# Cross-attention of the last layer: where VectorE joins, normalises and carries the first batch of a pair

## The reference

```python
def _mha(x, y, ...):                      # second call: y = ee, causal=False
    xn = _ln(x, lnx_g, lnx_b)
    yn = _ln(y, lny_g, lny_b)
    q = jnp.einsum('bsc,hcd->bhsd', xn, wq)
    ...
    a = jax.nn.softmax(jnp.einsum('bhsd,bhtd->bhst', q, k) * D ** (-0.5), axis=-1)
    o = jnp.einsum('bhst,bhtd->bhsd', a, v)
    ...
    x_out = x + o @ li1_w + li1_b
    h = jax.nn.gelu(_ln(x_out, ln3_g, ln3_b) @ li2_w + li2_b, approximate=False)
    return x_out + h @ li3_w + li3_b
...
x = _ln(x, ln2_g, ln2_b)
return x + _mha(x, ee, a2_wq, ...)
```

## Time and profile before

| what | value |
|---|---|
| median of 3 runs | 3002.09 us (2995.72 to 3003.3) |
| the profiled execution's own time | 3003.06 us |
| its span in the trace | 3001.4 us |
| PE busy | 2444.2 us (81%) |
| DVE busy | 1303.4 us (43%) |
| ACT busy | 889.5 us (30%) |
| POOL busy | 683.4 us (23%) |

### The profile page before, as it was taken

The page is one execution under the profiler, slowest core; times in us unless marked ns, Lnnn a source line. Parts: engine busy times, 40 slices in busy tenths (PEclk is TensorE's granted clock), DMA queues, the critical chain, the costliest instruction groups (busy, mean ns, idle before and its releaser), DMA issues.

```text
span 3001.4 us, 32215 instructions
## 1 busy us (share of the span) xinstructions
PE 2444.2 (81%) x11498; PEld 1621.5 (54%) x11498; DVE 1303.4 (43%) x2740; ACT 889.5 (30%) x1980; POOL 683.4 (23%) x767
## 2 busy tenths in 40 slices
PE   6898888987688299977899799999783299999925
PEld 3555554555366177753446554446462168888703
DVE  6664465634555311115673536573526023333205
ACT  3453254533341022213553225562310011111100
POOL 3052220122012400013111320002311702222270
PEclk9899999998798599988999899999795699999967
DMA  9000000000002322200000000000001315555430
GB/s 361 16 1 1 1 1 1 1 1 0 7 1 106 143 88 94 95 32 14 15 15 1 0 1 1 1 1 1 1 0 74 117 57 197 197 199 197 142 101 28
DMA packets 64402, 173.28 MB, mean 58 GB/s; under 512 B 6608, under 2 KB 45136, under 8 KB 56208
## 3 DMA queue, kind: packets, MB, share of 16 engines
q0 software_dynamic: 21280, 95.11, 9.2%
q1 hardware_dynamic: 43008, 76.66, 7.1%
HBM read 121.81 MB, written 49.94 MB: 57 GB/s over the span
## 4 chain that ended last, share of the span: by engine, by line
PE 70%; DVE 13%; another core or an unknown queue 5%; issue 5%; ACT 4%; POOL 2%; DMA 0%; DVEq 0%; ACTq 0%; SPq 0%; POOLq 0%
PE PS L2175 8%; PE PS L982 6%; PE PS L973 6%; PE PS L576 5%; PE PS L1950 5%; PE PS L1964 5%; PE PS L2189 4%; PE PS L606 4%; PE PS L932 3%; PE PS L517 3%; PE PS L556 2%; PE PS L2090 2%; DVE arena L680 2%; PE PS L1162 2%
## 5 line engine op out<-in xcount | busy, mean ns | idle before, releaser
L637 ACT ACTIVATE arena<-PS,arena 128x512 f32<-128x512 f32 (+3 forms) x512 | 306.4, 606 | 207.5 <-DVE arena L680 173.1
L680 DVE TENSOR_REDUCE arena<-PS 128x1 f32<-128x512 f32 (+3 forms) x512 | 273.4, 584 | 137.3 <-PE PS L582 82.9
L576 PE MATMUL PS<-arena 64*128 64x512 f32 (+3 forms) x1024 | 294.6, 567 | 32.4 <-ACT arena L637 21.8
L2175 PE MATMUL PS<-arena 128*128 128x256 f32 (+1 forms) x1128 | 252.1, 379 | 0.9 <-DVE arena L2213 0.9
L2175 PEld LDWEIGHTS PS<-arena 128*128 128x128 f32 (+1 forms) x1128 | 203.4, 180 | 40.7 <-issue 1.1
L288 POOL TENSOR_TENSOR arena<-arena 128x4 f32<-128x4 f32 x45 | 47.6, 1057 | 761.1 <-DVE arena L299 370.9
L2090 PE MATMUL PS<-arena 128*128 (+1 forms) x192 | 96.8, 661 | 142.4 <-issue 93.6
L606 PE MATMUL PS<-arena 128*128 128x128 f32 x1280 | 174.1, 281 | 17.0 <-ACT arena L637 12.8
L576 PEld LDWEIGHTS PS<-arena 64*128 64x128 f32 x1024 | 104.0, 187 | 143.9 <-ACT arena L637 93.9
L606 PEld LDWEIGHTS PS<-arena 128*128 128x128 f32 x1280 | 140.9, 144 | 71.7 <-ACT arena L637 47.3
L861 POOL TENSOR_TENSOR arena<-arena 128x512 f32<-128x512 f32 (+2 forms) x108 | 88.9, 827 | 381.2 <-ACT arena L832 375.6
(11 more groups left out here) (344 smaller groups left out, 3967.9 us busy)
## 6 DMA issues: line engine op xcount, KB each, us to landing
arena<-e SPq DMA_DIRECT2D x8, 2048.0 KB
arena<-slots SPq DMA_DIRECT2D x55, 256.0 KB, 2.7
yslots<-arena POOLq DMA_DIRECT2D x55, 256.0 KB, 7.8
slots<-zeros SPq DMA_DIRECT2D x1, 12032.0 KB, 39.6
slots<-zeros SPq DMA_DIRECT2D x1, 5120.0 KB, 34.9
arena<-w3a SPq DMA_DIRECT2D x1, 4106.0 KB, 13.5
arena<-w3b SPq DMA_DIRECT2D x1, 3593.0 KB, 21.6
arena<-slots SPq DMA_DIRECT2D x8, 384.0 KB
```

Of the source, the lines that this page charges most:

```text
L576: ins = nc.tensor.matmul(PS[:, hh, 0:w], q[:, t * P:(t + 1) * P], k[:, 0:w], start=True, stop=not cfg["causal"])
L637: nc.scalar.activation(PRB[m % 6][:, 0:w], PS[:, hh, 0:w], ACT.Exp, bias=nmax[:, m:m + 1], accum_out=rsum[:, col:col + 1]).then_inc(s["pro ...
L680: nc.vector.tensor_reduce(nmax[:, m:m + 1], PS[:, hh, 0:w], AX, ALU.max, negate=True).then_inc(s["nmax"], 1)
L2175: ins = nc.tensor.matmul(PS[0:n, 2 * c + up, 0:BN], wbuf3[i][:, off:off + n], xsT3[i][:, k, :], start=k == 0, stop=k == KC - 1)
```

## The change

In batch z's cross-attention (and in what follows it) VectorE's list is changed in four ways. The join of batch a stands ahead of the first shift, not behind it. The second shift is ahead of the moments. The normalisation of batch a is VectorE's own, behind the fourth shift (`third_scaled`), and that of batch z is too. `carried(a)` stands behind the sum of batch z. GpSimd keeps only the power of -0.5 for the two, without a wait for the sums.

```diff
--- before.py
+++ after.py
@@ -2522,9 +2522,9 @@
                 pool_norm(pool, N3("f2", z))
                 biased(1, z, "a2li1b", "a2li3b")
                 folded(z, range(1))
-                third(1, a)
+                pool_norm(pool, N3("f3", a))
                 folded(z, range(1, QT))
-                third(1, z)
+                pool_norm(pool, N3("f3", z))
                 if a + 2 < B:
                     pool_norm(pool, N3("ln1", a + 2))
                     scaled("f0", 0, a + 2, tiles_of(x1s[0]), xns[0])
@@ -2595,6 +2595,14 @@
                 x1 = x1s[b % 2]
                 V.tensor_tensor(x1, x1, xns[b % 2], ALU.add).then_inc(own["summed"], 1)
                 v.wait_ge(own["summed"], X3(stage, b) + 1)
+
+            def third_scaled(b):
+                v.wait_ge(norm["rstd"], N3("f3", b) + 1)
+                to = xns[b % 2]
+                for t in range(QT):
+                    ins = V.tensor_scalar(to[:, t, :], to[:, t, :], mv[:, 2 * t:2 * t + 1], rstd[:, t:t + 1],
+                                          ALU.subtract, ALU.mult)
+                ins.then_inc(xf["xn_ready"], 1)
 
             def carried(b):
                 xr = X[:, b * QT:(b + 1) * QT, :]
@@ -2663,20 +2671,22 @@
                 turned_x(2, z, c3c)
                 dve_cross_y(v, sc_, a + 2 * B, c3c, ch)
                 dve_cross_q(v, sc_, z + 2 * B, c3c)
+                joined(2, a)
                 shift(z, 0)
-                joined(2, a)
+                shift(z, 1)
                 third(1, a)
-                shift(z, 1)
                 summed(1, a)
                 shift(z, 2)
-                carried(a)
                 shift(z, 3)
+                third_scaled(a)
                 dve_cross_shares(v, sc_, z + 2 * B, c3c, ch, folds3)
                 turned_x(3, a, c3g)
                 dve_cross_y(v, sc_, z + 2 * B, c3c, ch)
                 joined(2, z)
                 third(1, z)
                 summed(1, z)
+                carried(a)
+                third_scaled(z)
                 turned_x(3, z, c3g)
                 carried(z)
                 if a + 2 < B:
```

## The result

| | before | changed |
|---|---|---|
| median, 7 runs each | 3001.44 us (2995.72 to 3003.3) | 2990.18 us (2984.78 to 2991.28) |
| ratio | | 0.9959, 95% interval 0.9948 to 0.997 |
| profiled execution, its span | 3003.06, 3001.4 us | 2984.78, 2983.1 us |
| first shift to feed-forward (L885 to L973), first pair | 31.87 us | 25.27 us |
| the same, second pair | 32.13 us | 25.13 us |

The account below looks back on a forecast made before the run. Bound taken: VectorE's last shift waiting for GpSimd's fold behind its scalings, on the ending chain twice. Earlier shifts 13.0 plus clock 2.0 gave 15.0 us off 3003.06; median 2987.0 us, range 2980 to 2995 (0.80).

Parts of the forecast that it names:

- The fold behind the scalings: Batch z's cross-attention: GpSimd's fold of tile 1, queued behind four scalings (5.87 us), holds VectorE's last shift.
- The join: VectorE, moved ahead of the first shift into idle time: gain 0 to 0.1 us, taken as 0.
- The last shift: VectorE, batch z's cross-attention: starts 6.5 to 7.2 us earlier, taken as 6.9; second pair 6.0 to 7.2, taken as 6.1.
- the base of the sum: Gain from the earlier last shifts in both pairs: 6.9 + 6.1 = 13.0 us.
- The scaling on VectorE: Scalings at 408 ns, at most 1.6 us per batch, covered: cost 0; contention bounds 1.2 (power), 1.6 us (folds or scalings).
- the shares' slack: VectorE finishes batch a's shares 2.25 us before TensorE turns them, covering the scalings.
- The clock: TensorE's last turns and features may stay at the high clock: 0 to 1.7 us a pair, taken as 2.0 in all.
- The rest: carried and batch z's scaling, now behind batch z's sum, have 8.0 us of cover under TensorE's feed-forward: cost 0.
- The sum: Whole kernel: 13.0 + 2.0 = 15.0 us less, giving a median of 2987.0 us.
- the lower bound of the range: Least total gain over two pairs: 2 x (6.0 - 0.7) = 10.6 us.
- Rival 1: Engines' round bounds; contention costs 1.2 (power) plus 1.6 (folds, scalings) a pair, no clock gain: 2995 us, chance 0.13.

Follow-up runs that it names:

- e2: Changed kernel with both batches' scalings back on GpSimd, between its folds of tile 0 and tile 1: 2999.97 us, 0.9991 of the kernel before.
- e3: Kernel before, with GpSimd folding tile 1 ahead of batch a's power and scalings, tile 2 behind them: 2990.89 us, 0.996 of the kernel before.
- e1: Kernel before with only the scalings moved from GpSimd to VectorE, the order of join, shifts, moments, sum and carried kept: 2995.19 us, 0.9977 of before.
- e9: e8 plus unread matmuls (0, 0, 4, 5) in TensorE's waits of batch a's cross-attention: 2980.97 us, 0.9937 of the kernel before.
- e8: Changed kernel plus unread matmuls (3, 0, 3, 1) in TensorE's four waits of batch z's cross-attention: 2983.82 us, 0.9934 of the kernel before.
- e4: Changed kernel with VectorE's sum of batch a moved behind the fourth shift, ahead of the scaling: 2985.78 us, 0.9942 of the kernel before.
- e7: Changed kernel's VectorE order, scalings left on GpSimd, its fold of tile 1 ahead of power and scalings: 2989.03 us, 0.9955 of the kernel before.
- e0_again: The changed kernel run again without edits: 2983.87 us, 0.9937 of the kernel before.

## Why the prediction was right, and where it was off

- **The fold behind the scalings.** Right, and shown: e2 keeps it and keeps the chain, e3 takes only it away and GpSimd no longer holds the last shift.
- **The join.** Cost next to 0, as said: it ended 0.48 us before the first shift, which starts 0.07 us later behind the scores. The possible small gain was 0: TensorE's first turns started 3.72 us behind the shift, as before.
- **The last shift.** 10.49 us reckoned for VectorE, 10.38 measured in the first pair. For the second 11.8 by TensorE's scores at the low clock, 10.80 measured, still released by the scores: they took 1.25 us and not 2.08. So the last shifts came 7.3 and 6.9 us earlier, 14.2 us where the base of the sum had 13.0; the first of them lies just above the bounds of 6.5 to 7.2.
- **The scaling on VectorE.** Cost 0, since the shares' slack held at the low clock. The contention was there, under the bounds of 1.2 and 1.6 us: the power took 1.93 for 1.03, the scalings 2.01 and 1.84 for 1.38. In e1, where GpSimd was idle at that moment, the scalings took 1.37 us. The Trainium skill (SBUF — State Buffer, Who interferes with whom) has tensor_scalar and copy among the VectorE instructions that can contend with GpSimd. The traces agree for both, with these scalings and with the copies of the shares in e9; the trace before did not show it. But the cost fell on time that nobody waited for, until e8 and e9 used that time up.
- **The clock.** This is the term that failed: 2.0 us put down, and the stretch from the last shift to the feed-forward became 0.6 us longer instead (14.89 and 14.33 us, before 14.17 and 14.42). The prediction said that the clock might stay high because "the waits left are shorter than the 4.43 us that went before a low clock". They were 3.08 and 1.32 us before the last two turns, and the clock was at 0.50 from 1724.0 to 1729.9 all the same. The length of the last wait doesn't sort the traces: turns behind 2.89 us (e3, first pair) and 2.08 us (e4, second pair) took 1.07 and 1.06 us, turns behind 0.78 us (e7) took 1.94. The first four values took 1.98 us in the first pair (1.33 in the same place before), a piece that the term had left out. And e8 shows the upper bound of 1.7 us a pair as too small: keeping the clock is worth 4.1 us in all, if TensorE is kept at work through its waits.
- **The rest.** Batch z's sum, carried and scaling ended at 1755.4, TensorE turned that batch at 1763.4: 8.0 us of cover, as reckoned, cost 0.
- **The sum.** 15.0 us forecast, 13.6 by the traces (14.2 earlier, less 0.6), 11.3 by the medians of 7 runs and 13.4 by all runs. The mechanism was right, but that the total came so close is partly luck: the base was 1.2 us too small and the clock's term 2.6 too large. The 0.7 us a pair in the lower bound of the range was never worked out from a row. Rival 1 named the contention rightly but not its price: both its parts were covered.

Left open: why the clock came back during the scores of tile 3 in the second pair and fell again before the last turns. In e0_again the two pairs have it the other way round, with the same code and waits within 0.2 us; the traces show the levels, not what sets them.

## What to carry to other kernels

When an engine's work is on the chain, ask first what is queued behind it: here a fold needed to get out from behind a scaling, and two ranges on GpSimd's list were worth about half of the change by the local distance. Remove a wait and read the next one on every engine at the clock that its waits leave it with; a shorter wait is not yet a high clock. Work put into a wait to hold the clock must be shorter than the wait, at its measured length. For an effect near the scatter of the runs, measure a distance inside the trace between two points that bracket the edit.

## What the runs showed of the hardware

- TensorE's granted clock was at 0.50 behind waits of 3.08 and 1.32 us between short turns, and stayed at 1.00 through the same stretch when matmuls that nobody reads stood in the waits (e8): 8 turns 1.06 us instead of 1.94, 4.1 us gained over two pairs.
- A VectorE copy of 128x512 in SBUF, 422 ns by the median, took 2574 ns at most in e9, beside a GpSimd addition of 2.59 us; four together 3.59 instead of 1.43. The harm goes both ways: a power of 4 columns on GpSimd took 1.93 us instead of 1.03 in all four places of the changed kernel, where VectorE's two-input sum had begun just before it, and 1.02 when the sum was moved away (e4).
